# Attention accumulates in two PSUM banks in turn, and the bank at rest takes the round's later steps

## The reference

```
q = xn Wq;  latent = (xn Wk + xn Wv) Wdown;  k = latent Wup_k;  v = latent Wup_v     (16 heads of 8)
scores = clip(q k^T * scale) * exp(-0.0001 |i - j|)      (512 x 512 per head)
attention = softmax(scores) v, heads joined, times Wo
experts: the best 2 of 8 by logits xn Wr^T + br, softmax over the two, gelu(xn W1^T + b1) W2^T + b2;
         plus xn, then a layernorm with ln_w, ln_b
```

## Time and profile before

| | |
|---|---|
| median of three runs | 242.39 us (242.2 to 244.27) |
| span of the profiled execution | 241.3 us |
| PE, PEld busy | 225.7 us (94%), 123.8 us (51%) |
| ACT, DVE, POOL busy | 196.7, 174.2, 186.3 us |
| attention's 128 exponentials on ACT (L1084) | 110.2 to 232.3 us |
| corrections (L1344), 128 | 69.1 us busy |
| outputs (L838), 512 products | 67.4 us busy |

### The profile page before, as it was taken

One profiled execution on the slowest core, in us unless ns is written; L12 is line 12 of the kernel. 1 busy time (PEld: TensorE's weight loads), 2 busy tenths in 40 slices (PEclk: granted clock), 3 DMA queues, 4 the chain that ended last, 5 costly groups with the idle time before them and its releaser, 6 DMA issues.

```text
span 241.3 us, 5128 instructions
## 1 busy us (share of the span) xinstructions
PE 225.7 (94%) x1704; PEld 123.8 (51%) x1704; DVE 174.2 (72%) x433; ACT 196.7 (82%) x374; POOL 186.3 (77%) x201
## 2 busy tenths in 40 slices
PE   7989699999989999997999999999989999999983
PEld 3945589999989999993322222221212222232222
DVE  1779667878888777786567877678777876867751
ACT  2496789866657666769999999999999999998951
POOL 7660489898886666896999999999889999999400
PEclk9979999999999999999999999999999999999998
DMA  6998115761237645614960156511556001001011
GB/s 182 465 400 374 33 35 199 287 236 46 87 106 211 159 124 145 182 46 143 258 137 22 33 146 171 155 35 24 159 157 173 1 4 43 1 3 43 1 46 48
DMA packets 18765, 30.88 MB, mean 128 GB/s; under 512 B 3104, under 2 KB 15296, under 8 KB 18480
## 3 DMA queue, kind: packets, MB, share of 16 engines
q1 hardware_dynamic: 16128, 25.61, 32.2%
q0 software_dynamic: 2272, 4.66, 7.9%
q10 hardware_dynamic: 336, 0.25, 0.4%
HBM read 13.27 MB, written 4.65 MB: 74 GB/s over the span
## 4 chain that ended last, share of the span: by engine, by line
PE 63%; ACT 18%; DVE 8%; issue 6%; DMA 3%; SPq 0%
ACT shared L1084 17%; PE ps L754 15%; PE ps L765 15%; PE ps L838 13%; PE ps L820 8%; DVE ps L1344 2%; PE ps L743 2%; DMA x_sb<-x_tiles 2%; PE ps L876 2%; PE ps L666 1%; DMA shared<-xn_scr,source_i 1%; PE ps L685 1%; PE ps L865 1%; DVE out_heads L1351 1%; PE ps L657 1%
## 5 line engine op out<-in xcount | busy, mean ns | idle before, releaser
L1084 ACT ACTIVATE shared<-ps 128x1024 f32<-128x1024 f32 x128 | 119.5, 1047 | 2.6 <-DVE ps L1344 1.8
L1344 DVE TENSOR_TENSOR ps<-ps,mend_sb 128x256 f32<-128x256 f32 (+1 forms) x128 | 69.1, 561 | 29.1 <-PE ps L820 23.7
L838 PE MATMUL ps<-shared,v_sb 128*18 128x512 f32 x512 | 67.4, 598 | 0.2
L395 POOL DMA_INDIRECT shared<-xn_scr,source_i x39 | 47.2, 1210 | 25.2 <-DVE source_i L1190 10.3
L1047 ACT ACTIVATE shared<-ps,shared 128x128 f32<-128x128 f32 x156 | 44.5, 368 | 20.1 <-PE ps L754 17.3
L820 PE MATMUL ps<-stacked 64*128 64x512 bf16 x256 | 47.6, 385 | 4.0 <-ACT shared L1084 2.7
L820 PEld LDWEIGHTS ps<-stacked 64*128 64x128 bf16 x256 | 12.3, 93 | 64.1 <-ACT shared L1084 45.4
L1208 DVE COPY shared<-panels 128x1156 f32 x37 | 34.2, 926 | 11.9 <-DVE y_rows L1269 7.5
L765 PE MATMUL ps<-shared 128*128 128x128 f32 x312 | 41.6, 276 | 0.7 <-issue 0.7
L754 PE MATMUL ps<-shared 128*128 128x128 f32 x312 | 41.6, 276 | 0.3 <-issue 0.3
L754 PEld LDWEIGHTS ps<-shared 128*128 128x128 f32 x312 | 38.2, 192 | 2.0 <-issue 1.5
(11 more groups left out here) (193 smaller groups left out, 260.6 us busy)
## 6 DMA issues: line engine op xcount, KB each, us to landing
panels<-weights SPq DMA_DIRECT2D x1, 4624.0 KB, 19.0
stacked<-parts SPq DMA_DIRECT2D x36, 128.0 KB
stacked<-early SPq DMA_DIRECT2D x36, 128.0 KB
stacked<-stacked SPq DMA_DIRECT2D x4, 768.0 KB
y_scr<-y_rows SPq DMA_DIRECT2D x19, 128.0 KB
x_sb<-x_tiles SPq DMA_DIRECT2D x4, 256.0 KB, 4.7
xn_scr<-x_sb SPq DMA_DIRECT2D x2, 512.0 KB, 8.5
panels<-x_tiles SPq DMA_DIRECT2D x1, 1024.0 KB
```

Of the source, the lines that this page charges most:

```text
L395: nc.gpsimd.indirect_dma_start(x_rows[:, i % X_SLOTS, :], None, xn_scr, bass.IndirectOffsetOnAxis(ap=source_i[:, i:i + 1], axis=0)).then_i ...
L838: last = nc.tensor.matmul(ps[32 * g:32 * g + 2 * VW, OUT_BANK, :], v_flat[:, at:at + 2 * VW], probs_fast[:, duo % DUO_SLOTS, g // 2, g % 2 ...
L1084: nc.scalar.activation(probs_fast[:, duo % DUO_SLOTS, couple, :, :], ps[:, score_bank(n):score_bank(n) + 2, :], ACT.Exp).then_inc(fast_pro ...
L1344: nc.vector.tensor_tensor(both, both, mend_sb[:, mends].unsqueeze(1).to_broadcast([P, 2, mends.stop - mends.start]), ALU.mult).then_inc(fa ...
```

## The change

The tables and constants. Numbers are units; a pair such as (22, 23) holds one for each half and repeats every 16 units.

```diff
-OUT_BANK, TURN_BANK = 6, 7
-OUTPUTS_AFTER, HEADS_AFTER, TURN_AFTER, NORMAL_AFTER = 4, 11, (13, 16), (15, 18)
+OUT_BANKS, TURN_BANK, VALUE_BANK = (7, 6), 7, 6
+OUTPUTS_AFTER, HEADS_AT, TURN_AT, NORMAL_AT = 4, (22, 23), (23, 25), (24, 26)
+ROUND_UNITS = 16
...
-        STATS_AT = (62, 72, 86, 102)
-        TURN_PARTS = {45: (0, 0), 47: (0, 1), 77: (1, 0), 79: (1, 1), 113: (2, 0), 115: (2, 1)}
-        VALUE_PARTS = {7: (2, 0), 11: (2, 1), 15: (3, 0), 19: (3, 1)}
-        PROJECT_PARTS = {93: (0, 0), 95: (0, 1), 109: (1, 0), 111: (1, 1), 125: (2, 0), 127: (2, 1)}
-        AFTER_TURNED, AFTER_ADDED = {2: 2, 4: 4, 6: 6}, {5: 2, 6: 4}
+        STATS_PARTS = {62: (0, (0, 1)), 63: (0, (2, 3)), 80: (1, (0, 1)), 81: (1, (2, 3)), 97: (2, (0, 1)), 98: (2, (2,)), 99: (2, (3,)),
+                       105: (3, (0, 1)), 107: (3, (2,)), 108: (3, (3,))}
+        VARIANCE_AT = {64: 0, 82: 1, 100: 2, 109: 3}
+        TURN_PARTS = {43: ((0, 0),), 45: ((0, 1),), 75: ((1, 0),), 77: ((1, 1),), 107: ((2, 0), (2, 1))}
+        KEEP_PARTS = {46: (0, 0), 47: (0, 1), 78: (1, 0), 79: (1, 1), 108: (2, 0), 110: (2, 1)}
+        VALUE_PARTS = {5: (2, 0), 7: (2, 1), 11: (3, 0), 13: (3, 1)}
+        KEEP_VALUES = {8: (2, 0), 9: (2, 1), 14: (3, 0), 15: (3, 1)}
+        PROJECT_PARTS = {91: ((0, 0),), 93: ((0, 1),), 111: ((1, 0), (1, 1)), 123: ((2, 0),), 125: ((2, 1),)}
+        PROJECT_ROUNDS = (4, 5, 6)
+        ADD_PARTS = {94: (0, 0), 95: (0, 1), 112: (1, 0), 113: (1, 1), 126: (2, 0), 127: (2, 1)}
+        ADDED_BEFORE = {6: 2, 7: 4}
```

Round r accumulates in out_bank(r), 7 or 6 in turn. The transposes of a round, the turning back behind an odd round and the products with Wo go into the bank whose round has ended; the values go into bank 6 during round 0. On PE:

```diff
+                def bank_free(round):
+                    if round == 0:
+                        pe.wait_ge(v_ones, 2)
+                        pe.wait_ge(out_clear, 1)
+                    elif round == 1:
+                        pe.wait_ge(v_ready[B - 1], 2)
+                    else:
+                        pe.wait_ge(fast_done, 2 * (round - 1))
+                        if round % 2:
+                            pe.wait_ge(attnT_ready, round - 1)
+                        if round in ADDED_BEFORE:
+                            pe.wait_ge(out_ready, ADDED_BEFORE[round])
...
                 def turn(round, half):
-                    pe.wait_ge(fast_heads, round + 1)
-                    if round or half:
-                        pe.wait_ge(fast_done, 2 * round + half)
-                    else:
-                        pe.wait_ge(v_ready[B - 1], 2)
...
+                    if half:
+                        pe.wait_ge(fast_done, 2 * round + 1)
+                    else:
+                        pe.wait_ge(fast_heads, 2 * (round + 1))
...
                 def turn_part(b, half):
...
+                    round = 2 * b + 1
+                    if half == 0:
+                        pe.wait_ge(fast_done, 2 * (round + 1))
...
                 def project_part(b, half):
...
+                    round = PROJECT_ROUNDS[b]
+                    if half == 0:
+                        pe.wait_ge(fast_done, 2 * (round + 1))
+                        pe.wait_ge(attnT_ready, round + 1 if round % 2 else 2 * (b + 1))
```

The first outputs of a round call bank_free instead of waiting for the heads' copy of the round before. The second halves of turned and projected parts, and of values, no longer wait for DVE to have read the first halves; DVE's copies and sums wait for both halves instead. On DVE the heads' copy is made in halves, and all extra pieces stand behind the correction of their unit:

```diff
-                def heads(round):
+                def heads(round, half):
+                    queries = slice(half * HALF, (half + 1) * HALF)
                     v.wait_ge(fast_used, 2 * QT * (round + 1))
                     if round:
-                        v.wait_ge(fast_outT, 2 * round)
-                    nc.vector.tensor_copy(out_heads[:], ps[:, OUT_BANK, :]).then_inc(fast_heads, 1)
+                        v.wait_ge(fast_outT, 2 * (round - 1) + half + 1)
+                    nc.vector.tensor_copy(out_heads[:, queries], ps[:, out_bank(round), queries]).then_inc(fast_heads, 1)
...
                 add_bias(WORK - 2)
                 mend(0)
+                v.wait_ge(y_read, WORK - 1)
+                nc.vector.memset(ps[:, out_bank(0), :], 0.0).then_inc(out_clear, 1)
                 add_bias(WORK - 1)
                 mend(1)
-                v.wait_ge(y_read, WORK)
-                nc.vector.memset(ps[:, OUT_BANK, :], 0.0).then_inc(out_clear, 1)
-                for n in range(UNITS + 4 * GROUP):
-                    if (round := round_at(n, HEADS_AFTER)) is not None:
-                        heads(round)
-                    if 2 <= n < UNITS:
-                        mend(n)
+                for n in range(2, UNITS):
+                    mend(n)
                     for half in range(2):
-                        if (round := round_at(n, NORMAL_AFTER[half])) is not None:
+                        if (round := round_at(n, HEADS_AT[half])) is not None:
+                            heads(round, half)
+                        if (round := round_at(n, NORMAL_AT[half])) is not None:
                             normalise(round, half)
```

More of the change, by code:

```diff
@@ L678, in value_part @@
             def value_part(b, half):
-                if b == 2 and half == 0:
-                    pe.wait_ge(y_read, WORK)
-                else:
-                    pe.wait_ge(v_ready[b - 1 + half], 2 - half)
+                if half == 0:
+                    if b == 2:
+                        pe.wait_ge(y_read, WORK)
+                    else:
+                        pe.wait_ge(v_ready[b - 1], 2)
                 for t in (2 * half, 2 * half + 1):
-                    last = nc.tensor.matmul(ps[:, TURN_BANK, t * P:(t + 1) * P], tokens_by_dim(b)[:, t * P:(t + 1) * P], wvl[:],
+                    last = nc.tensor.matmul(ps[:, VALUE_BANK, t * P:(t + 1) * P], tokens_by_dim(b)[:, t * P:(t + 1) * P], wvl[:],
                                             start=True, stop=True)
@@ L826, in outputs @@
                     pe.wait_ge(fast_probs, 2 * (duo + 1))
-                    second = group % 2
+                    round, second = divmod(group, 2)
                     if tile == 0 and not second:
[L829 to L833, removed]
+                        bank_free(round)
                     for g in range(GROUP):
@@ L837, in outputs @@
                         at = ((b * QT + tile) * HEADS + h) * 2 * VW - second * VW
-                        last = nc.tensor.matmul(ps[32 * g:32 * g + 2 * VW, OUT_BANK, :], v_flat[:, at:at + 2 * VW],
+                        last = nc.tensor.matmul(ps[32 * g:32 * g + 2 * VW, out_bank(round), :], v_flat[:, at:at + 2 * VW],
                                                 probs_fast[:, duo % DUO_SLOTS, g // 2, g % 2, :],
@@ L869, in project_part @@
                 def project_part(b, half):
[L870 to L874, removed]
+                    round = PROJECT_ROUNDS[b]
+                    if half == 0:
+                        pe.wait_ge(fast_done, 2 * (round + 1))
+                        pe.wait_ge(attnT_ready, round + 1 if round % 2 else 2 * (b + 1))
                     for t in (2 * half, 2 * half + 1):
-                        last = nc.tensor.matmul(ps[:, TURN_BANK, t * D:(t + 1) * D], attnT[:, b * QT + t, :], wo_sb,
+                        last = nc.tensor.matmul(ps[:, out_bank(round), t * D:(t + 1) * D], attnT[:, b * QT + t, :], wo_sb,
                                                 start=True, stop=True)
@@ L884, in _ @@
                 narrow(WORK - 1)
-                for n in range(UNITS + 4 * GROUP):
+                for n in range(UNITS + OUTPUTS_AFTER):
                     if 2 <= n < UNITS:
@@ L891, in _ @@
                     for half in range(2):
-                        if (round := round_at(n, TURN_AFTER[half])) is not None:
+                        if (round := round_at(n, TURN_AT[half])) is not None:
                             turn(round, half)
@@ L895, in _ @@
                         value_part(*VALUE_PARTS[n])
[L896 to L899, removed]
+                    for part in TURN_PARTS.get(n, ()):
+                        turn_part(*part)
+                    for part in PROJECT_PARTS.get(n, ()):
+                        project_part(*part)
                 for half in range(2):
[L901 to L904, removed]
+                    pe.wait_ge(fast_heads, 2 * (ROUNDS - 1) + half + 1)
                     for t in (2 * half, 2 * half + 1):
@@ L1310, in _, with token_stats @@
                         split_left(b, LEFT_STEPS.index(n - start))
-            def token_stats(b):
-                v.wait_ge(acc_ready, b + 1)
-                for t in range(b * QT, (b + 1) * QT):
+            def token_stats(b, places=range(QT)):
+                if places[0] == 0:
+                    v.wait_ge(acc_ready, b + 1)
+                for t in (b * QT + place for place in places):
                     last = nc.vector.bn_stats(stats[:, t, :], acc[:, t, :])
-                then(last)
+                if places[-1] == QT - 1:
+                    then(last)
             def token_variance(b):
@@ L1399, in _ @@
                         weigh()
[L1400 to L1412, removed]
+                    if n in STATS_PARTS:
+                        token_stats(*STATS_PARTS[n])
+                    if n in VARIANCE_AT:
+                        token_variance(VARIANCE_AT[n])
```

(9 more changed lines are left out.)

41 lines of the change are left out of this document (15 added, 26 removed).

## The result

The changed kernel takes **250.0 us** (median of four runs, 249.94 to 250.43) against 242.29 (median of four, 242.05 to 244.27): 1.0322 times as long, 95% interval 1.0289 to 1.0356. The profiled execution took 250.06 us, of which 248.4 are the span.

The account below looks back on a forecast made before the run. ACT's exponentials were taken to set the attention stage's pace, with 4.6 us of waits. Waits after summed to 12.7, 8.0 more, added to the median 242.39: 250.4 us, range 246.5 to 252.5.

Parts of the forecast that it names:

- The stop: At PE's unit 23 the turn waits for the second heads copy: 1.26 us from scores to turn, PE standing 0.94.
- What a round loses: ACT's loss per round from stop and turns: 0.72 us at unit 25, 0.44 at 27, together 1.16.
- The other parts: Waits after the change: values 1.1 us, rounds 0 and 2 1.16 each, 1 and 3 1.39, 4 and 6 1.83.
- Round 5: Both halves of a turn at 107 and of a product at 111 add losses; the round's waits 2.8 us.
- The old copy's cost: Heads copy ahead of a long correction: 0.2 us in six rounds, 0.6 in the seventh; its removal takes away 1.8.
- DVE's pieces: Half copies and statistics by twos cost nothing, fitting into DVE's idle 0.88 or 0.61 us before an odd unit's correction.
- POOL: Waits some 3 us longer for the first variance, ends near 230 instead of 226.13, and costs nothing.
- Rivals 1 and 2: Wait at the turn hidden: either only the old copy's cost goes (239.5 us, 5%), or pieces cost as counted (243.2, 7%).
- rival 2: PE's wait at the turn is hidden and the pieces cost as counted: 243.2 us; chance 7%.
- Rival 3, the clock: PE's clock falls at the rounds' stops, 1.7 us of PE's time each, seven making 12 more: 262 us; chance 3%.
- The span: The profiled span of 241.3 us becomes 249.3, by 8.0 us more waits.

Follow-up runs that it names:

- v2: Changed kernel with copies, turns, normalisations, value parts, turned parts, products and split statistics moved to places counted as free; 241.32 us, ratio 0.9968 to the kernel before.
- e1: Changed kernel with both half copies of the heads behind the correction of unit 22; 243.72 us, ratio 1.0097 to the kernel before.
- e2b: Changed kernel with one more DVE statistics instruction before the second half copy in rounds 0 to 6; 252.12 us, ratio 1.0407.
- v4: v2 with weighing at 32, statistics by fours, batch 2's turned part at 107 and batch 1's product whole at 111; 239.63 us, ratio 0.9895 to the kernel before.
- v3: v2 with weighing at 16, statistics by fours, batch 0's products one tile at a time, batch 1's three and one; 241.32 us, ratio 0.9958.
- e3: Changed kernel with PE's value parts, turned parts and products of batches 0 to 2 cut to 8 columns, for timing only; 245.7 us, ratio 1.016.

## Why the prediction was right, step by step

The mechanism held in each step, and the sum 8.0 came out as 7.55 in waits and 7.7 in time.

- **The stop.** 0.44 to the correction, 0.34 to the copy, 0.47 to the turn: 1.25, predicted 1.26, of which PE stood 0.93 (0.94). It was built from three rows of other places, and these carried over.
- **What a round loses.** 1.13 against 1.16. The 0.72 put at unit 25 shows as 0.31 at 24 and 0.39 at 25, since the scores of 24 are late too; the 0.44 at 27 as 0.04 and 0.39. In this kernel 0.39 or 0.40 is the most that one odd unit loses; why there is such a limit was not asked. The prediction had the sum of a round right; its split was off, since units 24 and 26 lose time too.
- **The other parts**, predicted and measured: values 1.1 and 1.15; rounds 0 and 2 1.16 and 1.13; rounds 1 and 3 1.39 and 1.40; rounds 4 and 6 1.83 and 1.84.
- **Round 5 was mis-sized**: 2.8 and 2.29. I took four tiles as twice two. The time line around 216 and 221 us of the changed kernel:

```profile
216.61 0.66 PE L875 MATMUL ps<-chain_sb,qT_sb 128*128 128x128 f32 x4
...
217.20 0.39 PE L828 MATMUL ps<-stacked 64*128 64x512 bf16 x2
...
220.70 1.13 PE L885 MATMUL ps<-rest_sb,kT_sb 128*128 128x128 f32 x8 [0.29 <-DVE kT_sb L1383]
...
221.76 0.39 PE L828 MATMUL ps<-stacked 64*128 64x512 bf16 x2
```

  From a piece's start to the next scores: four transposes 0.59 (twice 0.37 was counted), a product of four tiles 1.06 (twice 0.64). That is 0.15 and 0.22 less, and the 0.11 put on the next correction did not occur: 0.48 of the 0.51.
- **The old copy's cost**: no loss at units 19, 35, 51 and so on any more, and the exponential of unit 2 loses nothing to the memset. Both gains are there and are outweighed, as counted.
- **DVE's pieces** by halves and twos cost nothing in the changed kernel. That v2's statistics did at 74 and 90, places I chose, shows that this cover is a property of the place.
- **POOL** waited 3.0 us for the first variance and then finished in time (its last instruction ends at 229.54, near 230 as predicted).
- **Rivals 1 and 2** needed the turn to find its copy made. e1 is that kernel: 243.72, against 243.2 for rival 2.
- **Rival 3, the clock.** The stretch from 131 us to the last exponential, to be set beside the earlier trace rows (the columns are the same):

```profile
131.00:239.70 108.70, 98.53 (x702) 24.06 (x698) 77.52 (x207) 101.47 (x107) 88.34 (x103) 1.00 0.23 64
```
  
  The granted clock is 1.00, the 2.4 GHz level, through all seven stops, and in e2b's stops of 1.18 it is 1.00 as well. (The last digit of PEclk above is a fall at the span's end, behind the stage; the kernel before has the same digit there, and the prediction did not name it.) The Trainium skill (TensorE: Matmul & The Clock Gate, HAM oscillation) tells of a kernel whose clock fell in each of its pauses, which were waits for DMA several times as long as the stops here. The prediction was too broad in reading it as a forecast for a stop of 0.94; the trace shows no fall at stops of this size.
- **The span** came out at 248.4 instead of 249.3: 0.5 is round 5, and 0.4 is a first exponential 0.16 earlier and an end 0.24 shorter, which I had taken as unchanged.

## What to carry to other kernels

Where engines run in order and one sets the pace, work out for each place in the loop how late the feeder may be before the pacing engine stops (here 0.12 or 0.39 us), and what it regains per turn; moved work is then a sum. Freeing a buffer earlier wins nothing if the new wait stands on the feeder's queue and what it waits for is itself behind the feeder's latest output: put a piece's producer at least one unit ahead of the unit at which its consumer is issued. Of the 7.7 us, 6.3 came from one copy placed one unit too late (e1); what is left shows as losses behind turns and other pieces. v4, with two banks and other places, took 1% less than the kernel before.

## What was not expected of the hardware

**A piece on PE has a fixed part.** From its start to the next scores an fp32 product took 0.42 with one 128x128 tile, 0.65 with two (226.87 to 227.52), 0.84 with three (211.71 to 212.55; all of v3) and 1.06 with four (changed kernel): some 0.2 each, and 0.2 once. Cutting a piece smaller costs that part again, which v3 paid.

**A small DVE instruction ended with POOL's.** The weighing's first instruction, 128x16, from SBUF to SBUF, took between 0.17 and 1.36 us in the eight traces. Beside it stands the end of the POOL instruction that was running then (in v3 POOL's began 0.04 after DVE's):

| kernel | DVE from, length | DVE's end | POOL's end |
|---|---|---|---|
| before | 137.81, 0.67 | 138.48 | 138.44 |
| changed | 138.92, 0.49 | 139.41 | 139.38 |
| e1 | 137.82, 0.27 | 138.09 | 138.04 |
| e3 | 137.59, 0.53 | 138.12 | 138.08 |
| e2b | 138.78, 0.17 | 138.95 | 138.89 |
| v2 | 137.82, 1.13 | 138.95 | 138.92 |
| v3 | 124.19, 1.36 | 125.55 | 125.51 |
| v4 | 139.32, 0.25 | 139.57 | 139.57 |

It ends up to 0.06 behind POOL's in all eight, whether POOL's was a TENSOR_TENSOR or the issue of a gather. The Trainium skill (SBUF — State Buffer, SBUF: two separate sides) says that DVE, in some of its instructions, and POOL share a pair of ports that one holds for its whole instruction while the other is blocked; the traces agree with it. Not every DVE instruction is held: the TENSOR_TENSOR of 128x16 two places behind it took 0.17 in v2 (139.28), inside the issue of POOL's next gather (139.07 to 140.03). No run took POOL's instruction away, so the cause is argued from the ends and the page, not shown by an experiment. The largest single losses of v2 and v3, 0.63 and 0.94 us, stand behind this instruction.
